# Cross-attention and a quantized feed-forward on one core: first scores ahead of the last context keys, the usual path of PE in straight line, and a bias added by PE

## What is computed

```
x:   (1, 2048, 256)   ctx: (1, 1601, 256)   mask: (1, 1601), true only for the last keys (at most 400 of them)
# cross-attention, 4 heads of 64; the "latents" are the rows of layernorm(x)
xn = layernorm(ctx) * g + b            ; ln = layernorm(layernorm(x)) * g' + b'
q  = ln @ W_q                          ; kv = concat([xn @ W_kv, ln @ W_kv])
qn = rmsnorm(q) * q_gamma / 8          ; kn = rmsnorm(k) * k_gamma      (per head)
attn = softmax(where(mask or own row, qn @ kn.T, -inf))
x  = x + (attn @ v) @ W_out + b_out
# feed-forward with quantized activations and weights, hidden size 1024
h  = bit_linear(layernorm(x), w1)      ; h = silu(depthwise_conv1d(h, conv_w) + conv_b)
x  = x + bit_linear(h, w2)
```

## Time and profile before

| what | value |
|---|---|
| three runs | 479.63, 480.08 and 477.93 us, median 479.63 us |
| the profiled execution | 480.25 us, span from first to last instruction 478.2 us |
| busy share of the span | PE 87%, DVE 82%, ACT 65%, PEld 59%, POOL 16% |
| mean granted TensorE clock | 0.968 of full speed |
| projections, attention, feed-forward | about 0 to 90, 90 to 377 and 377 to 478 us |

### The profile page before, as it was taken

How to read it: one execution, slowest core, us unless ns; L and a number is a source line. 1 busy time by engine, 2 the same in 40 slices (tenths; PEclk the granted TensorE clock), 3 DMA queues, 4 the chain that set the end, 5 groups by cost and what they waited for, 6 DMA issues and landing times.

```text
span 478.2 us, 15103 instructions
## 1 busy us (share of the span) xinstructions
PE 415.0 (87%) x5910; PEld 282.9 (59%) x5910; DVE 391.1 (82%) x635; ACT 313.0 (65%) x359; POOL 78.3 (16%) x93
## 2 busy tenths in 40 slices
PE   0999985489999999999699899899899977798876
PEld 0666664146666666666476566666576644565664
DVE  4389999299978789879669878889878899999964
ACT  1356675156697766666556656656756567889866
POOL 2075554560000111010102002002001010000000
PEclk9999999599999999999999999999999995999989
DMA  8700000521211211111111111111111000010001
GB/s 231 183 1 1 1 2 10 179 94 45 67 46 35 68 35 45 58 35 45 48 36 45 56 36 45 58 34 45 41 33 42 1 0 2 0 45 23 24 24 66
DMA packets 27447, 22.56 MB, mean 47 GB/s; under 512 B 7229, under 2 KB 26878, under 8 KB 27390
## 3 DMA queue, kind: packets, MB, share of 16 engines
q1 hardware_dynamic: 25978, 21.72, 14.2%
q10 hardware_dynamic: 1412, 0.01, 0.2%
HBM read 7.04 MB, written 2.10 MB: 19 GB/s over the span
## 4 chain that ended last, share of the span: by engine, by line
PE 49%; DVE 21%; issue 14%; ACT 13%; ACTq 2%; DMA 1%; DVEq 1%
PE sc L1355 13%; DVE arena L698 7%; PE heads L1372 6%; PE heads L1373 5%; PE heads L1374 5%; ACT arena L1083 4%; PE heads L1251 3%; PE sc L1260 2%; PE by L1408 2%; ACT qq L1166 2%; ACT qq L1158 1%; DVE arena L592 1%; PE by L1528 1%; PE sc L1511 1%; PE heads L1511 1%
## 5 line engine op out<-in xcount | busy, mean ns | idle before, releaser
L698 DVE SCALAR_TENSOR_TENSOR arena<-arena 128x1024 bf16<-128x1024 f32 x160 | 196.2, 1260 | 40.3 <-ACT arena L1083 39.9
L1083 ACT ACTIVATE arena<-sc,kb 128x1024 f32<-128x1024 f32 x160 | 170.2, 1113 | 90.0 <-PE sc L1355 89.8
L1372 PEld LDWEIGHTS heads<-v,arena 128*128 128x128 bf16 x1280 | 117.7, 97 | 47.2 <-issue 34.2
L1372 PE MATMUL heads<-v,arena 128*128 (+1 forms) x1280 | 131.0, 194 | 10.3 <-DVE arena L698 8.9
L1355 PE MATMUL sc<-qs,kst 64*128 64x512 f16 x960 | 121.0, 385 | 11.7 <-issue 9.9
L1373 PE MATMUL heads<-v,arena 128*128 (+1 forms) x1280 | 129.6, 195 | 0.0
L1374 PE MATMUL heads<-v,arena 128*128 (+1 forms) x1280 | 129.0, 193 | 0.0
L1374 PEld LDWEIGHTS heads<-v,arena 128*128 128x128 bf16 x1280 | 119.1, 99 | 0.0
L1373 PEld LDWEIGHTS heads<-v,arena 128*128 128x128 bf16 x1280 | 118.9, 98 | 0.3
L1355 PEld LDWEIGHTS sc<-qs,kst 64*128 64x128 f16 x960 | 42.7, 95 | 59.2 <-issue 21.0
L470 POOL TENSOR_SCALAR frs<-fmv 128x2 f32<-128x2 f32 x8 | 7.0, 869 | 165.4 <-DVE fmv L750 165.4
(11 more groups left out here) (185 smaller groups left out, 590.5 us busy)
## 6 DMA issues: line engine op xcount, KB each, us to landing
kst<-kk SPq DMA_DIRECT2D x80, 128.0 KB, 2.0
xs<-in_x SPq DMA_DIRECT2D x8, 256.0 KB, 6.7
qs<-qq SPq DMA_DIRECT2D x16, 128.0 KB, 2.3
out<-cbuf SPq DMA_DIRECT2D x7, 256.0 KB, 2.1
xs<-in_ctx SPq DMA_DIRECT2D x6, 256.0 KB, 7.3
xs<-in_L_ffn_w SPq DMA_DIRECT2D x1, 1024.0 KB, 5.5
cbuf<-in_L_ffn_w SPq DMA_DIRECT2D x1, 1024.0 KB, 9.1
arena<-in_L_xattn_W_kv SPq DMA_DIRECT2D x1, 512.0 KB, 6.3
```

What stands on the lines that cost most here:

```text
L698: e.scalar_tensor_tensor(out=rest[:, j, :, :], in0=prob[:, j, :, :], scalar=SHRINK, in1=probh[:, j, :, :], op0=ALU.mult, op1=ALU.subtract) ...
L1083: a_.activation(prob[:, j, :, :], sc[j % 2][:, :, :], ACT.Exp, bias=kb[:, bass.ds(i * QUAD + j, 1)]).then_inc(exp_done[j], 1)
L1372: t_.matmul(o, hi, row[:, 0:OW], start=first and sub == 0, stop=False, skip_group_check=True)
```

## The change

It moves the first scores ahead of the last two pairs of keys, takes `cc` out of a loop and writes its three rounds out, puts the usual path first in PE's code, with a copy of the head of the feed-forward (`first_block`) in both branches, and adds the bias by a matmul with three rows (a float16 split of `b_out` in three parts) instead of by POOL.

```diff
-        bout = sb("bout", [P, D], F32)
+        bout = sb("bout", [3, 2, D], F32)
+        bparts = sb("bparts", [3, 4, D], F16)
...
@@ projections (all engines): turns 8 and 9 leave it
-            turn(nq * 2 - 2, None, None, None, C, C, None, 0)
-            turn(nq * 2 - 1, None, None, None, None, C, C, 1)
-            finish(nq * 2 - 1, C)
...
@@ SP
-            sp.wait_ge(s["kl_ready"], XP)
-            sp.wait_ge(s["ql_ready"], XP)
+            sp.wait_ge(s["kl_ready"], 2)
+            sp.wait_ge(s["ql_ready"], 2)
             for g in range(HP):
                 stage_queries(0, g)
             stage_keys(0, 0, 0, True)
-            sp.wait_ge(s["kl_ready"], nq * 2)
-            sp.sem_inc(s["passed"], 1)
+            sp.wait_ge(s["kl_ready"], XP)
+            sp.wait_ge(s["ql_ready"], XP)
             sp.wait_ge(s["z_ready"], nq * 2 + 2)
             ... the loads of w1 and w2 ...
+            for i in range(1, XP // 2):
+                stage_keys(0, i, i)
+            sp.wait_ge(s["kl_ready"], nq * 2)
+            with sp.Fori(XP // 2, nq) as i:
+                stage_keys(0, i, i)
...
@@ POOL
+            heads_scale(nq * 2 - 1, H)
-            with pool.Fori(0, T // 2) as b:
-                add_bias(b)
+            def split_bias():          # 10 operations on 3 partitions x 256
+                ...
+            split_bias()
...
@@ DVE
+            def last_keys(i):
+                n = nq * 2 - 2 + i
+                slots = kk[:, :, bass.ds(2 * n, 2), :, :]
+                src = pk_late[i].rearrange("p t g c -> p g t c")
+                dve.wait_ge(s["qkt_ready"], n + 1)
+                e.tensor_copy(slots[:, :, :, 0, :], src).then_inc(s["kc_ready"], 1)
+                dve.wait_ge(s["kc_ready"], i + 1)
+                e.tensor_tensor(slots[:, :, :, 1, :], src, slots[:, :, :, 0, :], ALU.subtract).then_inc(s["kl_ready"], 1)
+            normed_heads(nq * 2 - 2, H, 0)
+            squares(nq * 2 - 1, H)
             with dve.If(unsafe(dve) > 0):
                 ...
+            with dve.Else():
+                remainder(0, 0)
+                last_keys(0)
+                remainder(0, 1)
+                normed_heads(nq * 2 - 1, H, 1)
+                remainder(0, 2)
+                last_keys(1)
+                remainder(0, 3)
...
-            with dve.Fori(0, nq - 4) as i:
+            with dve.Fori(1, nq - 3) as i:
                 remainders(i)
-            for q in range(4):
-                ... one of four sums in each of the last four quads
+            for q in range(3):
+                ... one sum in each of the last three, and two in the last
-            dve.wait_ge(s["xb_ready"], T // 2)
...
@@ ACT
             nq = projections(act, turn, finish)
+            evacuate(nq * 2 - 1, H, 1)
+            square(nq * 2 - 1, H, 1)
...
@@ PE
+            def last_keys(i):
+                n = nq * 2 - 2 + i
+                pe.wait_ge(s["qkn_ready"], n + 1)
+                ... 4 transposes into pk_late[i]
             pe.wait_ge(s["ql_ready"], XP)
+            pe.wait_ge(s["kl_ready"], nq * 2 - 2)
+            pe.wait_ge(s["raw_ready"], nq * 2)
...
@@ quad of unit 0, before its first values
+                    pe.wait_ge(s["kl_ready"], nq * 2 - 1)
+                    pe.wait_ge(s["vlo_ready"], nq * 2)
...
@@ out_project, and late_project in the same way
+                pe.wait_ge(s["bias_ready"], 1)
                 for t in range(2):
+                    t_.matmul(rows_bank(b)[1][:, t * D:(t + 1) * D], one16[0:3, :], bparts[:, 3, :], start=True, stop=False)
                     for k in range(KD):
-                        ... start=(k == 0)
+                        ... start=False
...
@@ attention
                 score(0, 0, 0, 0, shifted, True)
                 score(0, 0, 0, 1, shifted)
+                if not shifted:
+                    last_keys(0)
                 for hp in range(HP):
                     base = nq * hp
-                    if hp == 0:
-                        all_operands()
-                    quad(0, hp, hp, base, 0, True, None, shifted)
+                    quad(0, hp, hp, base, 0, True, None, shifted, (last_keys, 1) if hp == 0 and not shifted else None)
...
-                with pe.Fori(0, NCH - 2) as cc:
-                    unit(cc, 0, (cc + 1, 1))
-                    unit(cc, 1, (cc + 2, 0))
-                with pe.Fori(NCH - 2, NCH - 1) as cc:
-                    unit(cc, 0, (cc + 1, 1))
-                    unit(cc, 1, ())
+                for cc in range(NCH - 1):
+                    unit(cc, 0, (cc + 1, 1))
+                    unit(cc, 1, (cc + 2, 0) if cc < NCH - 2 else ())
...
-            with pe.If(find_largest > 0):
-                largest_scores()
-                attention(True)
-            with pe.Else():
-                attention(False)
+            with pe.If(find_largest < 1):
+                attention(False)
+                first_block()      # hidden(0, 0) to hidden(1, 2), the lines that stood here
+            with pe.Else():
+                largest_scores()
+                attention(True)
+                first_block()
             late_rows_first(0)
             hidden_edges(1)
```

More of the change, by code:

```diff
@@ L252, in xattn_ffn @@
         pk = bank[5].rearrange("p (t g c) -> p t g c", t=2, g=HP)
+        pk_late = [pk, bank[6].rearrange("p (t g c) -> p t g c", t=2, g=HP)]
         hb = [bank[2], bank[3], bank[6]]
@@ L671, in _ @@
                                           bank[1][0:1, 0:P]).then_inc(s["shift_ready"], 1)
+                for j in range(QUAD):
+                    remainder(0, j)
+            with dve.Else():
+                remainder(0, 0)
+                last_keys(0)
+                remainder(0, 1)
+                normed_heads(nq * 2 - 1, H, 1)
+                remainder(0, 2)
+                last_keys(1)
+                remainder(0, 3)
             def weights_summed(n):
@@ L1289, in _ @@
             find_largest = unsafe(pe)
+            def last_keys(i):
+                n = nq * 2 - 2 + i
+                pe.wait_ge(s["qkn_ready"], n + 1)
+                pe.sem_inc(s["passed"], 1)
+                for t in range(2):
+                    for g in range(HP):
+                        last = t_.transpose(pk_late[i][:, t, g, :], qkn[:, t, H + 2 * g:H + 2 * g + 2, :].rearrange("p e d -> p (e d)"), ident[:, :])
+                last.then_inc(s["qkt_ready"], 1)
             def weights_total():
@@ L1383, in quad @@
                     wait(pe, "heads_done", unit)
+                if first and isinstance(unit, int) and unit == 0:
+                    pe.wait_ge(s["kl_ready"], nq * 2 - 1)
+                    pe.sem_inc(s["passed"], 1)
+                    pe.wait_ge(s["vlo_ready"], nq * 2)
+                    pe.sem_inc(s["passed"], 1)
                 values(hp, n, i, 0, first, False)
@@ L1542, in late_project @@
                 for t in range(2):
+                    t_.matmul(rows_bank(b)[1][:, t * D:(t + 1) * D], one16[0:3, :], bparts[:, 3, :], start=True, stop=False)
                     for k in range(KD):
[L1544 removed]
+                        last = t_.matmul(rows_bank(b)[1][:, t * D:(t + 1) * D], ot_late[i][:, t, k, :], wout[:, k, :], start=False, stop=(k == KD - 1))
                 last.then_inc(s["y_ps"], 1)
@@ L1555, in late_rows_first, with first_block @@
                 last.then_inc(s["xd_ps"], 1)
-            hidden(0, 0)
-            hidden(0, 1)
-            hidden(0, 2)
-            hidden_edges(0)
-            late_heads_first(0)
-            late_heads_first(1)
-            hidden(0, 3)
-            late_project(0)
-            hidden(0, 4)
-            hidden(0, 5)
-            late_project(1)
-            hidden(0, 6)
-            hidden(0, 7)
-            hidden(1, 0)
-            hidden(1, 1)
-            hidden(1, 2)
+            def first_block():
+                pe.wait_ge(s["xd_ready"], NB - 2)
+                pe.wait_ge(s["pad_done"], 1)
+                hidden(0, 0)
+                hidden(0, 1)
+                hidden(0, 2)
+                hidden_edges(0)
+                late_heads_first(0)
+                late_heads_first(1)
+                hidden(0, 3)
+                late_project(0)
+                hidden(0, 4)
+                hidden(0, 5)
+                late_project(1)
+                hidden(0, 6)
+                hidden(0, 7)
+                hidden(1, 0)
+                hidden(1, 1)
+                hidden(1, 2)
+            with pe.If(find_largest < 1):
[5 more added lines that the diff above has]
+                first_block()
             late_rows_first(0)
```

68 lines of the change are left out of this document (43 added, 25 removed).

## The result

The changed kernel takes 476.02 us (median of 6 runs, 475.50 to 478.12) beside 479.24 us (6 runs, 477.93 to 480.08) of the kernel before on the same chip: a ratio of 0.994, 95% interval 0.9922 to 0.9959. It is faster by 3.2 us where 9.6 were forecast, and lies 1 us above the upper end of the range. The profiled execution took 476.18 us with a span of 474.1; the forecast for it was 470.65.

The account below looks back on a forecast made before the run. PE was taken to set the pace, DVE close behind. Terms -8.1 + 0.8 - 4.2 + 1.3 + 0.2 + 0.4 = -9.6 us on the profiled 480.25 gave 470.65, so a 470.0 us median; range 465.5 to 475.0 us.

Parts of the forecast that it names:

- part 4: Bias on PE in the out projection: +1.3 us over six units, and +0.2 us in the late projections.
- part 5: Jump over the general path, now behind first_block, mostly hidden before the late rows: +0.4 us (0 to 1.5).
- Part 2: Quad 2 to quad 5: two weight sums in one quad, four sums instead of three on DVE, +0.8 us (0 to 1.2).
- Part 1: Between projections and attention: first scores before the last keys, quad 2 starts earlier, -8.1 us (bounds -10.5 and -4.5).
- Rival 3: Start gains half: DVE's jump costs 4 us, keys wait longer, POOL blocks DVE; 473.5 us, chance 0.12.
- Part 3: Between attention units: no loop over cc, so no wait at its back-edge, -4.2 us (bounds -4.2 and -3.4).
- Rivals 4 and 6: Seam between rounds stalls as the loop did, 474.2 us, chance 0.06; written-out quads pause for instruction fetch, slower, chance 0.04.
- Rival 2: New jump's wait is exposed before the late rows, costing PE 3.4 us and 0.8 of clock; 473.8 us, chance 0.12.

Follow-up runs that it names:

- the last experiment: Changed kernel with one 512-column bias matmul over 128 rows, 128 never-executed instructions and weight sums back behind remainder 1, against the kernel before: 467.73 us, ratio 0.9767.

## Why the prediction was wrong, point by point

The direction was right and its size was not: the forecast was -9.6 us on the profiled execution, it came to -4.1, or -3.1 without the 1.0 us of chance at the start. That leaves 6.5 us. Two steps hold most of them: the price of a bias matmul in part 4, which had the right mechanism and the wrong size, and in part 5 the moment from which the wait at the jump was counted as over. Part 2 adds the rest.

- **Part 1, right in its gain, by luck in its first mark.** First scores at 82.19 us (forecast 82.5), scores of quad 1 at 90.47 (92.1), of quad 2 at 97.96 (100.0). Without the 1.0 us the gain is 9.1 against 8.1, inside its bounds. But the first scores were due at 83.2 without it: DVE's last q_low ended at 81.04 us instead of 82.06, and from there to the scores PE took 1.15 us (1.1 to 1.2 in every kernel with the change), not the 0.44 I had allowed for its waits and flag. PE stood 3.4 us, not 2.7. DVE's jump didn't show: it did its first remainder at 84.40 us, 1.6 sooner than I had it, and the clock was low for 3.4 us, not through quad 1. Rival 3 falls.
- **Part 2, mis-sized**: +2.1 us up to the first unit (63.69 in place of 61.59) instead of +0.8, above its bound of 1.2. The fourth sum costs about what I counted, 1.0 us as the last experiment leaves it (62.61 - 61.59). The other 1.1 us come from the order, which I didn't cost: the sum moved from behind remainder 1 to ahead of it, and PE's values wait for remainder 1.
- **Part 3, right.** The seams show no gap; the kernel with the loop back is 6.9 us longer at that place. Rivals 4 and 6 fall: written-out units run at 35.28 us without the bias.
- **Part 4, mis-sized, the largest term.** 0.73 us in place of 0.22 in each of six units, and 1.1 in place of 0.2 in the late projections, which aren't hidden under DVE's queue: 5.6 us in place of 1.5. Another 0.3 us of that stretch are there without bias too, in none of my terms, and their cause is open. The row I took the price from is eight matmuls of one shape in a run. In the stream a 3-row matmul stands between 128-row ones, and that costs about 0.1 us at each of three starts, its own and those of the two matmuls behind it. My upper end, "twice as much, if a change of operand type costs as much again", named the wrong cause and was too low. The Trainium skill (TensorEngine Tiling (Array Packing), Key Properties) says that changing the tiling mode drains the engine; the runs agree as far as they show the number of rows to be the cause, and put a size to it; that it is this drain they don't show.
- **Part 5, the step whose mechanism failed**: +2.9 us in place of +0.4. The jump itself is hidden as I argued: its record ends at 393.80 us, and the late rows start at 394.07, 1.14 us after the work before them, the same as with no gap. But I had treated the wait as over once the first instruction behind the join is there. The code of the next block comes later, and with the boundary 4 instructions behind the join PE runs dry. The Trainium skill (Runtime: NRT & Kernel Launch, Instruction fetch mechanics) has blocks of 256 instructions; the period in the runs, 192 more being 64 fewer, agrees. Rival 2 gave 473.8 us for an exposed wait and was the nearest case, though by another mechanism: the landing of the jump isn't late, what follows it is.

In sum the costs were put too low by 1.3 us in part 2, 4.1 in part 4 and 2.5 in part 5, and 0.3 were in no part; part 1 gained 1.0 us more than I said, and 0.6 at the end go with the clock fall that didn't come: 1.3 + 4.1 + 2.5 + 0.3 - 1.0 - 0.6 = 6.6, the 6.5 us within rounding.

## What to carry to other kernels

Price a small matmul by the distance between the starts of its neighbours, not by its columns, and give it as many rows as they have, filled with zeros. When PE jumps over a long stretch of code, look for an "issue" gap some instructions behind the target too: its length is set by where the code lies, and unexecuted padding ahead of the target can take it away. When an operation is moved in a full queue, the cost is that of whoever waits for the operation it now stands ahead of, even where the work is the same.

## What the runs showed of the hardware

- A change between matmuls over 128 rows and over 3 or 64 costs about 0.1 us each way (values behind 64-row scores start 0.31 us after the last of them, where 0.213 lie between two pairs). Before float32 matmuls it costs twice that on the way back, since the second of them is late too: 0.32 us instead of 0.216 behind the first. The 64-row scores behind the out projection pay it in the kernel before too: the last of its float32 matmuls starts at 174.70 us, the scores at 175.01, 0.31 us later, where 0.216 lie between two of the float32 ones.
- A long jump of PE took 3.3 to 3.8 us in its own record, in every kernel here that has one.
- A gap of PE on "issue" behind such a jump moved with the number of instructions ahead of it, executed or not: 2.8 us at 4 instructions behind the join, 2.06 at 34, 0.8 and 0.6 at 66, 1.48 at 68 where PE had done its 34 matmuls at 2.4 GHz and so sooner, none where the count gives 132.
- Where the clock falls isn't the same in all runs of one kernel: the padded kernel's took 475.15 and 474.55 us at a granted clock of 0.978, 473.20 at 0.989 and 472.23 at 0.993. A change of 2 us in one stretch can be lost in that in the median, as with the kernel whose rest is in the branch.
